# The last block's shared expert on its 32 class rows alone, with another pace of gathers and another share of combines, in a vision-tower kernel on Trainium2

## The reference

```python
# xf: the LayerNorm of 32 x 257 rows of 256 elements
shared = silu(xf @ shared_w1.T) * (xf @ shared_w2.T) @ shared_w3.T      # hidden size 1024
scores = sigmoid(xf @ router_w.T)                                       # 8 experts
_, top_idx = top_k(scores + expert_bias, 2)
gates  = scores * one_hot(top_idx, 8).sum(-2)
h1, h2 = split(einsum('td,ehd->teh', xf, w12), 2)                       # routed hidden size 256
routed = einsum('teh,edh->td', silu(h1) * h2 * gates, w3)
out    = h + shared + routed
```

## Time and profile before

| | us |
|---|---|
| three timed runs | 2460.08, 2464.15, 2467.2 |
| their median | 2464.15 |
| the profiled execution | 2453.32 |
| its span (first to last instruction) | 2451.2 |
| TensorE busy in it | 2253.1 (92%) |
| VectorE busy | 1412.4 (58%) |
| ScalarE busy | 1005.7 (41%) |
| GpSimd busy | 685.2 (28%) |

### The profile page before, as it was taken

The page is one execution under the profiler, slowest core; times in us unless marked ns, Lnnn a source line. Parts: engine busy times, 40 slices in busy tenths (PEclk is TensorE's granted clock), DMA queues, the critical chain, the costliest instruction groups (busy, mean ns, idle before and its releaser), DMA issues. The chain is left out here.

```text
span 2451.2 us, 42478 instructions
## 1 busy us (share of the span) xinstructions
PE 2253.1 (92%) x15647; PEld 1888.5 (77%) x15647; DVE 1412.4 (58%) x3028; ACT 1005.7 (41%) x2074; POOL 685.2 (28%) x734
## 2 busy tenths in 40 slices
PE   3789999999999999999988799999999999999999
PEld 2567676776767767677665599999998888888998
DVE  6356666666666666666653344476664444444776
ACT  0124445454454544545444333322223555554332
POOL 3323323232232322323210211100002333332766
PEclk9689999999999999999997699999999999999999
DMA  2242432323234242342330333200002333333665
GB/s 76 35 65 48 80 56 65 73 48 77 56 68 73 48 77 55 69 73 48 66 57 20 134 129 130 100 27 27 19 27 80 96 95 96 96 95 86 180 181 161
DMA packets 125336, 189.42 MB, mean 77 GB/s; under 512 B 23153, under 2 KB 76418, under 8 KB 125138
## 3 DMA queue, kind: packets, MB, share of 16 engines
q1 hardware_dynamic: 102050, 135.52, 23.4%
q0 software_dynamic: 12736, 34.69, 5.7%
q10 hardware_dynamic: 10352, 16.52, 2.1%
HBM read 84.52 MB, written 49.58 MB: 55 GB/s over the span
## 5 line engine op out<-in xcount | busy, mean ns | idle before, releaser
L799 DVE TENSOR_REDUCE mx<-ps 128x2 f32<-128x514 f32 x512 | 351.0, 686 | 217.4 <-PE ps L455 217.4
L639 ACT ACTIVATE pT<-ps 128x514 f32<-128x514 f32 x512 | 306.8, 601 | 371.7 <-PE ps L472 368.1
L455 PE MATMUL ps<-km,q 112*128 112x258 f32 x1024 | 265.3, 341 | 91.5 <-DVE mx L799 80.2
L455 PEld LDWEIGHTS ps<-km,q 112*128 112x128 f32 x1024 | 164.0, 192 | 188.3 <-DVE mx L799 142.0
L1918 POOL DMA_INDIRECT z<-zd,itab x136 | 129.2, 950 | 515.9 <-DVE itab L1831 268.5
L472 PE MATMUL ps<-q,km 114*128 114x258 f32 x1024 | 232.1, 310 | 6.2 <-ACT pT L639 2.6
L1221 PE MATMUL ps<-zhi,whi 128*128 128x256 f32 x1056 | 217.8, 288 | 4.0 <-DVE wlo L1858 3.9
L1221 PE MATMUL ps<-zhi,wlo 128*128 128x256 f32 x1056 | 213.8, 284 | 0.0
L1221 PE MATMUL ps<-zlo,whi 128*128 128x256 f32 x1056 | 213.5, 284 | 0.0
L472 PEld LDWEIGHTS ps<-q,km 114*128 114x128 f32 x1024 | 165.4, 197 | 52.8 <-issue 31.5
L1249 ACT ACTIVATE sil<-ps 128x512 f32<-128x512 f32 x132 | 79.0, 598 | 282.2 <-PE ps L1221 282.2
(11 more groups left out here) (310 smaller groups left out, 4986.4 us busy)
## 6 DMA issues: line engine op xcount, KB each, us to landing
yd<-raws SPq DMA_DIRECT2D x136, 128.0 KB
q<-qhi SPq DMA_DIRECT2D x128, 129.0 KB, 4.2
km<-khi SPq DMA_DIRECT2D x256, 64.5 KB, 3.3
xs<-in_x SPq DMA_DIRECT2D x64, 256.0 KB, 4.5
z<-hscr SPq DMA_DIRECT2D x46, 256.0 KB, 3.0
raws<-in_wu SPq DMA_DIRECT2D x12, 768.0 KB, 4.6
hscr<-h SPq DMA_DIRECT2D x34, 256.0 KB, 5.1
zd<-z SPq DMA_DIRECT2D x33, 256.0 KB, 2.0
```

What stands on the lines that cost most here:

```text
L455: last = pe.matmul(ps[:, k, 0:NP], q2[p % U][0:MAXROW, QAT[g], t * P:(t + 1) * P], km[p % 2][0:MAXROW, k, g, :], start=True, stop=True)
L639: act.activation(pT[:, 2 * g:2 * g + 2, t, :], ps[:, score_bank(b, n):score_bank(b, n) + 2, 0:N], ACT.Exp, scale=HD ** -0.5).then_inc(s_ok, 1)
L799: dve.tensor_reduce(mx[:, t, 2 * QAT[g]:2 * QAT[g] + 2], ps[:, 0:2, 0:N], AX_X, ALU.max, negate=True).then_inc(mx_ok, 1)
```

## The change

Four edits. (1) For block 32 the moving side of `hidden`, and silu, product, head and split, take the first 32 columns of each half alone; `output` makes one tile of 32 rows; `total` adds these 32 rows. All other blocks are as before. (2) `paced(i)` becomes 4 * i // 13: thirteen gathers to a block. (3) `upto_x` gives blocks 17, 18, 19 to j = 9 (combined in units 1, 2, 3 of block 31) and 20, 21 to j = 10 (units 1, 2 of block 32). (4) As `JOBS` follows the shares, the last fetches go 17, 18, 19, 31, 20, 21, 32 instead of 17, 18, 31, 19, 20, 21, 32.

```diff
--- before.py
+++ after.py
@@ -1199,8 +1199,10 @@
                 last = pe.transpose(ps[:, 6, f * L + t * P:f * L + (t + 1) * P], z3[0][:, t, f * P:(f + 1) * P], eye[:])
         last.then_inc(t_ps, 1)
 
+    width = lambda k: L if k < B else B
+
     def hidden(pe, k, u, halves=(0, 1)):
-        p = k % 2
+        p, w = k % 2, width(k)
         if k == 0:
             pe.wait_ge(w_hi, u + 1)
             pe.wait_ge(w_lo, u + 1)
@@ -1218,7 +1220,7 @@
                 mm = [(w_, z_, f) for w_, z_ in ((whi, zhi[p]), (wlo, zhi[p]), (whi, zlo[p])) for f in range(FT)]
                 for n, (w_, z_, f) in enumerate(mm):
                     at = f * 2 * UH + m * UH + c * P
-                    last = pe.matmul(ps[:, 2 * (u % 2) + c, m * L:(m + 1) * L], w_[:, u, at:at + P], z_[:, f, :],
+                    last = pe.matmul(ps[:, 2 * (u % 2) + c, m * L:m * L + w], w_[:, u, at:at + P], z_[:, f, 0:w],
                                      start=(n == 0), stop=(n == len(mm) - 1))
             if c == 1:
                 last.then_inc(hid_ps, 1)
@@ -1231,11 +1233,12 @@
             pe.wait_ge(acc_ok, k)
         if u == 0 and k == XN:
             pe.wait_ge(y_ok, NT)
-        for t in range(LT):
+        tiles, w = (LT, P) if k < B else (1, B)
+        for t in range(tiles):
             mm = [(h_, w_, c) for h_, w_ in ((hhi, whi), (hlo, whi), (hhi, wlo)) for c in range(2)]
             for n, (h_, w_, c) in enumerate(mm):
                 at = FT * 2 * UH + c * D
-                last = pe.matmul(ps[:, 4, t * D:(t + 1) * D], h_[:, u % 2, c * L + t * P:c * L + (t + 1) * P],
+                last = pe.matmul(ps[0:w, 4, t * D:(t + 1) * D], h_[:, u % 2, c * L + t * P:c * L + t * P + w],
                                  w_[:, u, at:at + D], start=(n == 0 and u == 0 and t == 0),
                                  stop=(n == len(mm) - 1 and u == NS - 1), skip_group_check=True)
         last.then_inc(out_ps, 1)
@@ -1246,8 +1249,9 @@
             act.wait_ge(uu_ok, k * NS + u - 1)
         if k == XN and u < 2:
             act.wait_ge(xu_ok, NT)
-        act.activation(sil[:, u % 2, :].rearrange("p (c l) -> p c l", c=2),
-                       ps[:, 2 * (u % 2):2 * (u % 2) + 2, 0:L], ACT.Silu).then_inc(sil_ok, 1)
+        w = width(k)
+        act.activation(sil[:, u % 2, :].rearrange("p (c l) -> p c l", c=2)[:, :, 0:w],
+                       ps[:, 2 * (u % 2):2 * (u % 2) + 2, 0:w], ACT.Silu).then_inc(sil_ok, 1)
 
     def head(act, k, u):
         act.wait_ge(uu_ok, k * NS + u + 1)
@@ -1255,7 +1259,8 @@
             act.wait_ge(out_ps, k * NS + u - 1)
         if k == XN and u < 2:
             act.wait_ge(xy_ps, NT)
-        act.activation(hhi[:, u % 2, :], uu[:, u % 2, :], ACT.Copy).then_inc(hhi_ok, 1)
+        by_half = lambda t: t[:, u % 2, :].rearrange("p (c l) -> p c l", c=2)[:, :, 0:width(k)]
+        act.activation(by_half(hhi), by_half(uu), ACT.Copy).then_inc(hhi_ok, 1)
 
     def z_high(act, k):
         act.wait_ge(t_ps, k + 1)
@@ -1280,13 +1285,14 @@
         if k == XN and u < 2:
             dve.wait_ge(xh_ps, NT)
             dve.wait_ge(xhh_ok, NT)
-        dve.tensor_tensor(uu[:, u % 2, :].rearrange("p (c l) -> p c l", c=2),
-                          ps[:, 2 * (u % 2):2 * (u % 2) + 2, L:2 * L],
-                          sil[:, u % 2, :].rearrange("p (c l) -> p c l", c=2), ALU.mult).then_inc(uu_ok, 1)
+        w = width(k)
+        by_half = lambda t: t[:, u % 2, :].rearrange("p (c l) -> p c l", c=2)[:, :, 0:w]
+        dve.tensor_tensor(by_half(uu), ps[:, 2 * (u % 2):2 * (u % 2) + 2, L:L + w], by_half(sil), ALU.mult).then_inc(uu_ok, 1)
 
     def split(dve, k, u):
         dve.wait_ge(hhi_ok, k * NS + u + 1)
-        dve.tensor_tensor(hlo[:, u % 2, :], uu[:, u % 2, :], hhi[:, u % 2, :], ALU.subtract).then_inc(hlo_ok, 1)
+        by_half = lambda t: t[:, u % 2, :].rearrange("p (c l) -> p c l", c=2)[:, :, 0:width(k)]
+        dve.tensor_tensor(by_half(hlo), by_half(uu), by_half(hhi), ALU.subtract).then_inc(hlo_ok, 1)
 
     def tile_turn(pe, i):
 
@@ -1393,13 +1399,16 @@
         if k > 0:
             dve.wait_ge(acc_out, 16 * k)
         fl = lambda t: t[:].rearrange("p t d -> p (t d)")
-        dve.tensor_tensor(fl(acc), ps[:, 4, :], fl(hb[k % 2]), ALU.add).then_inc(acc_ok, 1)
+        if k < B:
+            dve.tensor_tensor(fl(acc), ps[:, 4, :], fl(hb[k % 2]), ALU.add).then_inc(acc_ok, 1)
+        else:
+            dve.tensor_tensor(acc[0:B, 0, :], ps[0:B, 4, 0:D], hb[k % 2][0:B, 0, :], ALU.add).then_inc(acc_ok, 1)
 
     GOT = LT * TOP * D
     yg = [raws[:, q * GOT:(q + 1) * GOT] for q in range(3)]
     hc = zx
     LAST = K - XN
-    upto_x = lambda j: XN if j == LAST else max(0, 2 * j - 1)
+    upto_x = lambda j: max(0, 2 * j - 1) if j < LAST - 1 else XN - 2 * (LAST - j)
     share = lambda j: range(upto_x(j), upto_x(j + 1))
     combined_at = lambda j, n: n + 1 if j > 0 else NS - 1
     JOBS = [c for j in range(LAST) for c in list(share(j)) + [XN + j]]
@@ -1918,7 +1927,7 @@
                 pool.indirect_dma_start(zg(i), None, zd_rows,
                                         bass.IndirectOffsetOnAxis(itab[:, i:i + 1], 0)).then_inc(zg_in[i % NG], 16)
 
-            paced = lambda i: i // 3
+            paced = lambda i: 4 * i // 13
 
             def fetch(c):
                 q = slot_of(c)
```

## The result

The changed kernel took 2496.31 us (median of 4 runs, 2487.66 to 2499.86); beside it the kernel before took 2462.11 us (4 runs, 2450.51 to 2467.2). The ratio is 1.0144, with a 95% interval of 1.0106 to 1.0182. The prediction was 2464.6 us and no change. It was wrong, and by more than any of its rivals reached.

What follows compares the result with a forecast made beforehand. TensorE was taken as the bound per block, with the last gathers level with it at the end. An earlier gather train but longer VectorE tail netted +0.5 us, added to the timed median 2464.15: 2464.6 us, range 2457 to 2470.

Steps and rivals of the forecast that it cites:

- Gathers thirteen to a block: Blocks 22 to 31: free buffers replace the pace's waits as the limit, TensorE hides everything; counted as zero.
- waits of VectorE in blocks 23 to 30 that reach TensorE: Shared-expert blocks before the end: a sign that would show the forecast wrong; no size given.
- 2.66 instead of 2.84 us a unit, a saving of 0.7 us in the block: Block 32's narrow `hidden`: 111 instead of 118 ns a matmul, since weight loads stay; saves 0.7 us.
- at 2.6 to 2.7 us a unit: Block 32's `hidden` on TensorE: its time per unit, a sign that the forecast is right.
- TensorE idle for some 7 us in block 32: Block 32: TensorE waits along with VectorE for landings, some 7 us; a sign that the forecast is right.
- The gather train: Last gathers on GpSimd: about 6 us idle, start 2421.71, i = 127 at 2441.4 instead of 2442.58, 1.2 us won.
- Waits for landings before 19, 31, 20 and 21: Blocks 31 and 32: VectorE waits for gathered rows before these four sums, about 1 us before 19.
- rival D: Block 32: narrow operands save TensorE nothing, and the time stays the forecast's; chance 0.68 together with the forecast.
- The tail behind combine 21: End of block 32: product, head, split, six matmuls, total and combine 32 follow block 21's sum, 3.4 us.
- rival C: End of block 32: TensorE's waits lower its clock, six matmuls cost 1.0 us more, 2465.6 us; chance 0.08.
- rival A: Block 32: landings come in time, the gathers don't hold the end; 5.6 us earlier, 2458.6 us; chance 0.10.
- B: Last gathers: stragglers and a late landing lengthen the train, +3.4 us, 2467.5 us in all; chance 0.14.

Runs made afterwards that it cites:

- e2: Kernel before with only the pace of thirteen gathers to a block (4 * i // 13), on chip 8: ratio 0.9991.
- e17: The whole change, unaltered, beside the kernel before on chip 8: 2451.86 against 2448.62 us, ratio 1.0007.
- e8: Kernel before with only the pace of thirteen gathers to a block, on chip 11: ratio 1.0128, two runs.
- e12: Kernel before with only the pace changed, to 12.5 gathers a block (8 * i // 25), on chip 11: ratio 1.0109.
- e13: Kernel before with no pace: all gathers free after the first unit, held only by their buffers, on chip 11: ratio 1.0192.
- e10: The changed kernel with the old pace i // 3, beside the kernel before on chip 11: ratio 0.9971.
- e11: The kernel before, unaltered, run for its trace on chip 11: 2448.64 us, one run.
- e15: Kernel before with twelve gathers a block freed all at once (4 * (i // 12)), on chip 1: ratio 0.9989.
- e16: Kernel before with twelve gathers a block freed all at once (4 * (i // 12)), on chip 8: ratio 1.0025.
- e18: Kernel before with twelve gathers a block freed all at once (4 * (i // 12)), on chip 12: ratio 0.998.
- e3: Kernel before with only the new shares: combines 17, 18, 19 under block 31 and 20, 21 under block 32, on chip 8: ratio 1.0015.

## Why the prediction was wrong, step by step

**The step that failed** is "*Gathers thirteen to a block.* [...] I count zero", with "TensorE hides everything" as its reason. That holds on chip 8 (e2, e17). On a late chip it is the whole result: with the pace alone the loss is there (e8, e12, e13: 1.1 to 1.9%), with everything but the pace it isn't (e10). The term counted as zero was 42.5 us over nine blocks in the changed kernel. The step missed what the old pace does there besides limiting the rate. It makes GpSimd wait for the very signals that come late under gathers: in e11 a late signal stopped the gathers after at most seven, in e10 after at most ten. Loosened by half a gather a block, that brake acts half as often. What holds GpSimd instead is VectorE's combines, which are themselves late because TensorE is: it is released all at once, runs a train of twelve, delays the signals by 5 to 6 us, and so makes the next release late too. That loop is a reading of the traces of e8 to e13, argued and not shown by a run of its own, and it says nothing of the pauses within TensorE's groups. What was shown by changing one thing is the part of the pace, on chip 11.

The prediction named the sign under which it would be wrong ("waits of VectorE in blocks 23 to 30 that reach TensorE"), and it came, but no rival stood behind it. The trace of before gave no hint of a size: every increment there was on time, even under a train of 28 gathers. A second trace of the kernel before, from another chip, would have shown it (e11: 0.93 us).

**A second step failed on every chip, and its time didn't show it:** "2.66 instead of 2.84 us a unit, a saving of 0.7 us in the block". The price of a narrow matmul was right at the full clock, but the clock wasn't kept, and the four units took 3.5 us more than the wide ones instead of 0.7 less. Of the signs named, `hidden` "at 2.6 to 2.7 us a unit" came for two units of four, and "TensorE idle for some 7 us in block 32" didn't come: it idled 0.39 of the 17.3 us before 2443.00. Its last `hidden`, with which it "would be done [...] at 2440", ended at 2444.46.

**The gather train, as worked out, held where signals are on time** (e17):
- GpSimd's idle time before the train: 6.3 us, to 2420.82; predicted some 6, to 2421.7.
- i = 127: 2441.03, fifteen steps at 1.35 us; predicted 2441.4 at 1.313.
- Waits for landings before 19, 31, 20 and 21: all four there, 1.6 to 2.6 us (before 19, 2.5 us where about 1 was predicted).
- Combine 21 ends at 2445.93 (predicted 2446.4), with product (32,3) directly behind.
- Narrow `hidden` at the full clock: pairs 0.22 us apart, so 111 ns a matmul, as the router's rows had it, and rival D falls as it was put. The formula of the Trainium skill's page "TensorE: Matmul & The Clock Gate", section "LDWEIGHTS (loading the stationary operand)", gives an estimate of 107 ns for 128 columns of load; the trace agrees within 4 ns.
- The tail behind combine 21: 3.8 us to the end of combine 32, predicted 3.4. Here rival C came true in part: the window 2443.00 to 2451.70 stands at 0.50 of the clock, which is 1.2 GHz, and the six matmuls take 1.48 us instead of 0.95. But the fall came within block 32's `hidden` units, sooner than C had it, and its ground, that TensorE waits, isn't borne out: the waits before it were 0.39 us.
- Against before the whole change is level there, as forecast. The train does hold the end, but by little: silu (32,3) was done at 2444.71, so product (32,3) was held 1.2 us by combine 21. Without the train the end would thus come some 1.5 us sooner (an estimate: these 1.2 us and the 0.39 that TensorE waited), and not the 5.6 of rival A.

The profiled execution of e17 took 2453.58 us where the prediction said 2453.8. So close a hit is luck: the eight runs of e17 lie between 2440.96 and 2461.67 us, and the sum held a TensorE that was done 4 us too soon.

**Rivals.** A moved the end by 8 us at most, B by 3.4. B had the sign right, but its mechanism, the landing of the last rows, plays no part: the loss is there before block 32 begins.

**What stays open.** Why an increment comes late, and TensorE pauses in mid-group, while GpSimd issues gathers, and why on some chips alone. Why the clock falls under the narrow block. Whether the length of a train or the mean rate does it: that late increments come just behind the end of a train speaks for its length, but no run on a late chip changed the one without the other, since e15, e16 and e18 met other chips. Whether the recording has a part: increments are missing from just those traces, and every time here is of a recorded execution.

## What to carry to other kernels

A pace that ties one engine to the signals of the slowest one is also a brake on whatever the two disturb in each other; price its loosening by what holds the engine next, and ask whether that keeps its work spread or releases it in bursts. Where a wait's releaser is unnamed on a one-core program, compare the signal's own time with the end of the instruction that gives it, before you believe any engine to be slow. A cost that one chip shows and another doesn't can't be read from one trace: take the kernel before on both. And where operands are made narrower, read the granted clock of the stretch before counting a saving.

## What the runs showed of the hardware

- TensorE's increments were seen 0.01 us behind the modelled end of their matmul on chips 1, 8 and 12, and 1 to 6 us behind it on chips 11 and 15 while GpSimd issued indirect gathers back to back (8.6 us at the most in e13, 14.8 under the changed kernel's train of seventeen). In those trains TensorE also paused within groups of matmuls that have no wait between them: 13.6 us in 170 in the changed kernel, 0.0 in e17.
- The traces with late increments hold 26,300 to 26,540 semaphore events, the others 30,811 to 30,818 for a program of the same size.
- With its own 128-column weight load and at the full clock, a matmul of this kernel takes 111 ns at 8 and at 32 moving columns and 118 ns at 256, so cutting the moving side saves next to nothing.
- TensorE's clock went from full to 0.50 (2.4 to 1.2 GHz) in a stretch of e17 in which it ran such narrow matmuls and was idle for 0.39 us; a narrow matmul then takes 213 ns. At 256 columns it stayed full through block 32, with idle time of 1.2 us (e3) and 1.4 us (e11).
